# Turning q tiles, weights and part of the probability tiles through memory in a split-precision attention kernel

## The chip, the core and the metric

The kernel runs on one core of a Trainium2 chip. The metric is the device time of one execution, in microseconds (us). The engines work side by side, each through its own queue in order: PE (TensorE) multiplies matrices and can turn (transpose) a 128x128 tile into PSUM; DVE (VectorE), ACT (ScalarE) and POOL (GpSimd) work on elements; SP only issues DMAs and waits. Engines and DMAs tell each other through semaphores that a piece of work is done. P is 128, the number of partitions.

## The reference

Two layers on x of 2 batches, 1024 tokens and 512 features, in float32: an attention block with 32 query heads and 8 key/value heads of width 128, then a mixture of eight low-rank adapters. Cut to what matters:

```python
x = x + attn(layernorm(x), Wq, Wk, Wv, Wo, q_norm_w, k_norm_w)
x = x + ffn(layernorm(x), A, B, Wr, br)
# attn
q = rmsnorm((x @ Wq.T) by heads, q_norm_w);  k = rmsnorm((x @ Wk.T) by heads, k_norm_w);  v = x @ Wv.T by heads
scores = q @ k.T / sqrt(128);  bias = slope * (key - query), or -1e30 where key > query
out = softmax(scores + bias) @ v @ Wo.T
# ffn
gate = 8 * softmax(x @ Wr.T + br);  out = 2 * sum over h of gate[h] * (x @ A[h].T) @ B[h].T
```

The mask is causal: of the 8 key tiles of 128 tokens, query tile s needs s + 1.

## The kernel before

**Precision.** Each operand of a large product is split into two parts, hi (rounded to a format that PE multiplies fast, F32R) and lo (the remainder), and a product is three matmuls: hi by hi, lo by hi, hi by lo (`split_product`, L920).

**Windows.** A window w is one batch and one key/value head with its four query heads: 8 windows for batch 0, 8 for batch 1. In the text an A window is an ordinary one of batch 0 (list `GROUP_A`), a B window an ordinary one of batch 1 (`GROUP_B`); `PROLOGUE`, `BOUNDARY`, `FIRST_B` and `LAST` are the others. In a window, stage s (0 to 7) is one query tile of 128 tokens with all four heads: `q.s.c` makes q in four parts (c = 0 to 3), `scores.s.h` the scores of head h against s + 1 key tiles, `max`, `exp`, `invert` and `normalise` the softmax, `values.s.j` the product with the values of key tile j, `y.s` the product with Wo, `add_y` the sum into y. `kv` makes k and v of the next window. In A windows the weights of the next head are loaded and made ready (hi and lo, contraction index on the partitions) and a copy is kept in memory; B windows fetch that copy.

**Turning.** A matmul needs its contraction index on the partitions, so q, k, the probabilities, the layer norm's output and the weights are all turned: `turn` (L932) does four PE transposes of 128x128 into one PSUM bank `turn_ps` (a ring of three), `high` on ACT (L625, or L627 with a scale) writes the hi part from the bank, `low` on DVE (L801, or L803 with a scale) the lo part. I call the four transposes a set. Probabilities take 36 sets a window, q 8, and in A windows the weights 10 more (2 for Wk and Wv, 4 for Wq, 4 for Wo).

**Order.** The order on every engine comes from the six lists of names at the top (`turn.p.4.2`, `q.6.1`, ...): each engine walks the same lists and does those names that are its own, with the waits that each name's function has (`follow`). Nothing is chosen at run time. All large DMAs are issued by SP, in that order too.

**Buffers that matter here.** `probs` holds two stages of unnormalised, then normalised probabilities; `qn` one q tile; `s_ps` (two PSUM banks) the scores, so that `scores` of a head waits for the `max` one or two heads back; `turn_ps` three sets.

## Time and profile before

| | |
|---|---|
| median of 3 runs | 2194.55 us (2194.45 to 2194.65) |
| the profiled execution | 2194.96 us, of which the span is 2193.1 us |
| mean granted TensorE clock | 0.995 |
| PE busy | 97% of the span |
| HBM traffic | read 69.75 MB, written 46.14 MB, 53 GB/s over the span |
| instructions in the span | 33323 |

The span runs from the first to the last instruction that the profiler recorded. Busy time is the union of an engine's instructions; matmuls overlap one another, so the mean duration of one is longer than its share of the engine. The chain that ended last is the better price of a matmul: it gives each instruction only the time by which it moved the end. The table of instruction groups names a group by the first operands of its shape, and a "(+7 forms)" means that its mean mixes shapes. A DMA's time to landing is from its issue to the last semaphore.

### The profile page before, as it was taken

To read this page: it belongs to the slowest core of one execution; us is meant where nothing else is said; L and a number is where in the kernel's file an instruction comes from. 1 tells how busy PE (TensorE), PEld (TensorE's weight loads), DVE (VectorE), ACT (ScalarE), POOL (GpSimd) and SP (SyncE) were. 2 spreads that over 40 slices of the span, in tenths; PEclk is the share of its full clock that TensorE was granted. 3 is DMA by queue.
4 is the path that set the end of the run, shared out by engine and by line. 5 is a ranking of instruction groups with operands and counts; after the bars stand their busy time and mean duration, and the time that the engine had idled before them with its cause. 6 is when DMAs were issued, how large, how long until landed. Compare 5 with 4: busy or idle time off the path is not lost.

```text
span 2193.1 us, 33323 instructions
## 1 busy us (share of the span) xinstructions
PE 2135.6 (97%) x12220; PEld 1834.4 (84%) x12220; DVE 1373.7 (63%) x3431; ACT 1149.2 (52%) x3314; POOL 802.1 (37%) x872
## 2 busy tenths in 40 slices
PE   7999999999999999999999999999999999999997
PEld 6888888888888888888888888888888888888885
DVE  5656656566565666669766556565556656565686
ACT  3555555465554655545545455454545545455542
POOL 2433424244242433424424344342424424243341
PEclk9999999999999999999999999999999999999999
DMA  4212111121210212111121011101001111101100
GB/s 173 87 58 87 59 57 46 43 87 58 87 58 1 87 58 78 63 38 65 58 97 39 20 39 39 59 39 59 2 38 58 39 58 39 44 15 39 39 15 24
DMA packets 32129, 118.01 MB, mean 54 GB/s; under 512 B 4185, under 2 KB 4185, under 8 KB 23777
## 3 DMA queue, kind: packets, MB, share of 16 engines
q1 hardware_dynamic: 31536, 115.89, 14.1%
q8 instruction: 98, 1.61, 0.3%
q14 instruction: 63, 0.51, 0.1%
q10 hardware_dynamic: 432, 0.01, 0.0%
HBM read 69.75 MB, written 46.14 MB: 53 GB/s over the span
## 4 chain that ended last, share of the span: by engine, by line
PE 91%; DVE 4%; ACT 2%; issue 1%; POOL 1%; DMA 0%; ACTq 0%; POOLq 0%; DVEq 0%
PE s_ps L923 26%; PE o_ps L923 18%; PE y_ps L923 16%; PE turn_ps L990 15%; PE q_ps L923 15%; DVE kT_lo L803 1%; DVE pT_lo L801 1%; PE y_ps L1079 1%; DVE oT_lo L848 1%; ACT qn L641 0%; ACT kT_hi L627 0%; ACT oT_hi L660 0%; PE turn_ps L984 0%; ACT pT_hi L625 0%; DVE low_gated L896 0%
## 5 line engine op out<-in xcount | busy, mean ns | idle before, releaser
L717 POOL TENSOR_TENSOR probs<-probs,p_inv 128x896 f32<-128x896 f32 (+7 forms) x512 | 578.0, 1150 | 784.8 <-DVE p_inv L821 784.5
L632 ACT ACTIVATE probs<-probs,neg_max 128x896 f32<-128x896 f32 (+7 forms) x512 | 396.6, 777 | 295.5 <-DVE neg_max L814 293.4
L814 DVE CUSTOM_DVE_ANT_0 probs<-s_ps,rel 128x896 f32<-128x896 f32 (+7 forms) x512 | 382.9, 753 | 268.1 <-issue 266.9
L625 ACT ACTIVATE pT_hi<-turn_ps 128x512 fp32r<-128x512 f32 x576 | 332.0, 597 | 308.6 <-PE turn_ps L990 308.5
L801 DVE TENSOR_TENSOR pT_lo<-turn_ps,pT_hi 128x512 fp32r<-128x512 f32 x576 | 384.6, 685 | 139.9 <-ACT pT_hi L625 138.8
L990 PE MATMUL turn_ps<-ident,probs 128*128 128x128 f32 x2464 | 343.7, 273 | 4.3 <-DVE probs L837 2.5
L990 PEld LDWEIGHTS turn_ps<-ident,probs 128*128 128x128 f32 x2464 | 295.1, 141 | 54.0 <-issue 5.4
L923 PE MATMUL s_ps<-kT_hi,qT_hi 128*128 128x512 f32 (+3 forms) x768 | 278.7, 363 | 14.1 <-DVE kT_lo L803 12.5
L923 PE MATMUL s_ps<-kT_hi,qT_lo 128*128 128x512 f32 (+3 forms) x768 | 263.1, 343 | 0.0
L923 PE MATMUL s_ps<-kT_lo,qT_hi 128*128 128x512 f32 (+3 forms) x768 | 261.8, 341 | 0.0
L923 PE MATMUL o_ps<-pT_hi,v_hi 128*128 128x512 f32 x576 | 243.2, 422 | 1.8 <-DVE pT_lo L801 1.7
L923 PE MATMUL o_ps<-pT_lo,v_hi 128*128 128x512 f32 x576 | 226.1, 393 | 0.0
L923 PE MATMUL o_ps<-pT_hi,v_lo 128*128 128x512 f32 x576 | 226.0, 392 | 0.0
L923 PE MATMUL q_ps<-wqT_hi,xnT_hi 128*128 128x512 f32 x512 | 220.8, 431 | 2.1 <-DVE qn L825 2.1
L923 PE MATMUL y_ps<-woT_hi,oT_hi 128*128 128x512 f32 x512 | 203.7, 398 | 4.7 <-DVE oT_lo L848 3.9
L923 PE MATMUL q_ps<-wqT_hi,xnT_lo 128*128 128x512 f32 x512 | 202.8, 396 | 0.0
L923 PE MATMUL q_ps<-wqT_lo,xnT_hi 128*128 128x512 f32 x512 | 201.9, 394 | 0.0
L923 PE MATMUL y_ps<-woT_lo,oT_hi 128*128 128x512 f32 x512 | 200.1, 391 | 0.0
L923 PE MATMUL y_ps<-woT_hi,oT_lo 128*128 128x512 f32 x512 | 200.0, 391 | 0.0
L641 ACT ACTIVATE qn<-q_ps 128x128 f32<-128x128 f32 x512 | 134.8, 278 | 95.9 <-PE q_ps L923 92.8
L923 PEld LDWEIGHTS s_ps<-kT_hi,qT_hi 128*128 128x128 f32 x768 | 145.0, 189 | 39.1 <-DVE kT_lo L803 16.1
L923 PEld LDWEIGHTS s_ps<-kT_lo,qT_hi 128*128 128x128 f32 x768 | 145.4, 189 | 19.3 <-issue 1.0
(105 smaller groups left out, 3621.1 us busy)
## 6 DMA issues: line engine op xcount, KB each, us to landing
wq_raw<-in_L_attn_Wq SPq DMA_DIRECT2D x8, 1024.0 KB, 5.6
wo_raw<-in_L_attn_Wo SPq DMA_DIRECT2D x8, 1024.0 KB, 6.0
wq_kept<-wqT_hi SPq DMA_DIRECT2D x8, 1024.0 KB, 5.0
wq_kept<-wqT_lo SPq DMA_DIRECT2D x8, 1024.0 KB, 7.2
wo_kept<-woT_hi SPq DMA_DIRECT2D x8, 1024.0 KB, 7.0
wo_kept<-woT_lo SPq DMA_DIRECT2D x8, 1024.0 KB, 9.1
wqT_hi<-wq_kept SPq DMA_DIRECT2D x8, 1024.0 KB, 4.8
wqT_lo<-wq_kept SPq DMA_DIRECT2D x8, 1024.0 KB, 6.9
```

The source lines that it names most:

```text
L625: nc.scalar.activation(target, bank, ACT.Copy).then_inc(sems["high"], 1)
L632: nc.scalar.activation(row, row, ACT.Exp, bias=neg_max[:, s % 2, h:h + 1], scale=-1.0, accum_out=p_sum[:, s % 2, h:h + 1]).then_inc(sems[" ...
L641: last = nc.scalar.activation(qn[:, h, :], q_ps[:, h * HD:(h + 1) * HD], ACT.Square, scale=float(slopes[gg % NG * G + h]), accum_out=q_sum ...
L717: nc.gpsimd.tensor_tensor(row, row, p_inv[:, s % 2, h:h + 1].to_broadcast((P, L)), ALU.mult).then_inc(sems["normalise"], 1)
L801: nc.vector.tensor_tensor(target, bank, upper.bitcast(F32), ALU.subtract).then_inc(sems["low"], 1)
L803: nc.vector.scalar_tensor_tensor(target, bank, scale, upper.bitcast(F32), ALU.mult, ALU.subtract).then_inc(sems["low"], 1)
L814: nc.vector.tensor_tensor_reduce(out=probs[:, s % 2, h, 0:L], in0=s_ps[:, at_col:at_col + L], in1=rel[:, S - L:S], scale=-float(slopes[w % ...
L848: nc.vector.tensor_tensor(oT_lo[:].rearrange(flat), o_ps[:], oT_hi[:].rearrange(flat).bitcast(F32), ALU.subtract).then_inc(sems["o_low"], 1)
L923: last = nc.tensor.matmul(target, a, m, start=start and i == 0 and k == 0, stop=stop and i == len(pairs) - 1 and k == 2)
L990: last = nc.tensor.transpose(bank[0:width, i * rows:(i + 1) * rows], source, ident[0:rows, 0:rows])
L1079: nc.tensor.matmul(y_ps[:], low_turned[:, t % 2, :], bT[:], start=True, stop=True).then_inc(sems["f_out"], 1)
```

## The change

1. **q.** `turn.q`, `high.q` and `low.q` go. In their place SP writes `qn` to a buffer in memory (`send_q`, one DMA) and reads it back with four DMAs (`fetch_q`), each for 32 partitions, in runs of 32 floats (128 bytes), such that the 32x32 blocks stand where the turned tile wants them; DVE turns each 32x32 block in place (`flip_q`, one instruction for 128x512), ACT writes hi (`upper_q`), DVE lo (`lower_q`), now both from SBUF.
2. **Probabilities.** 15 of the 36 tiles of a window (`MEMORY_TILES`: the last ones of stages 2 to 7) take the same way: `send_p` (one DMA for each head, after its `normalise`), `fetch_p` (four DMAs for one or two tiles), `flip_p` on DVE, `upper_p` on ACT, `lower_p` on POOL. The values product takes them last. The other 21 tiles are turned by PE as before.
3. **Weights.** They are loaded from the inputs already in blocks: Wq in 4 DMAs and Wk and Wv in 8, in runs of 512 bytes, Wo in 16 DMAs in runs of 128 bytes. `flip_w` on DVE, `upper_w` on ACT and `lower_w` on POOL make them ready. The loads of Wq, Wk and Wv and all DMAs that keep or bring back weights are issued by ACT; Wo's by SP. The three raw buffers become one (`w_raw`), so that each load waits for another weight's `lower_w`.
4. **Buffers.** Two slots of turned and three of fetched probability tiles; `probs` in two tensors, for even and odd stages; `max` of a stage waits until the stage two before it has been sent.
5. **Order.** All six lists are new.

The core of the diff:

```diff
--- before.py
+++ after.py
+MEMORY_TILES = {2: ((2,),), 3: ((2, 3),), 4: ((3, 4),), 5: ((3, 4), (5,)), 6: ((4, 5), (6,)), 7: ((4, 5), (6, 7))}
...
-    "turn.wo.0 high.wo.0 turn.wo.1 norm_q.1 high.wo.1 scores.0.0 low.wo.0 scores.0.1 turn.wo.2 max.0.0 q.2.0 max.0.1 "
+    "load_w.wkv scores.0.0 scores.0.1 norm_q.1 max.0.0 send_q.1 max.0.1 q.2.0 exp.0.0 flip_w.wo.0 exp.0.1 scores.0.2 "
...
+    TURN_SLOTS, MEMORY_SLOTS, RAW_PAIRS = 2, 3, 2
...
+    def through_memory(s):
+
+        return [j for group in MEMORY_TILES.get(s, ()) for j in group]
+
+    def values_order(s):
+        return [j for j in range(s + 1) if j not in through_memory(s)] + through_memory(s)
 
...
-        probs = sb("probs", [P, 2, G, S])
+        probs = [sb("probs_even", [P, G, S - P]), sb("probs_odd", [P, G, S])]
-        pT_hi = sb("pT_hi", [P, RING, G * P], F32R)
-        pT_lo = sb("pT_lo", [P, RING, G * P], F32R)
+        q_raw = sb("q_raw", [P, G * P])
+        p_raw = sb("p_raw", [P, 2 * RAW_PAIRS, G * P])
+        pT_hi = sb("pT_hi", [P, TURN_SLOTS + MEMORY_SLOTS, G * P], F32R)
+        pT_lo = sb("pT_lo", [P, TURN_SLOTS + MEMORY_SLOTS, G * P], F32R)
...
+        q_bounce = nc.dram_tensor("q_bounce", [2, G, P, HD], F32).ap()
+        p_bounce = nc.dram_tensor("p_bounce", [2, NT, G, P, P], F32).ap()
...
+            def send_q(w, n):
+                gg, s = w + n // NT, n % NT
+                unit = number["send_q", gg, s] - 1
+                if unit >= 2:
+                    sp.wait_ge(sems["flip_q"], unit - 1)
+                after(sp, "norm_q", gg, s)
+                sp.dma_start(q_bounce[unit % 2].rearrange("h p d -> p h d"), qn[:]).then_inc(q_sent, 16)
+
+            def fetch_q(w, n):
+                unit = number[named(w, "fetch_q", n)] - 1
+                sp.wait_ge(q_sent, 16 * (unit + 1))
+                if unit:
+                    sp.wait_ge(sems["lower_q"], unit)
+                blocks = q_bounce[unit % 2].rearrange("h (a j) (b i) -> b j (h a) i", j=BLOCK, i=BLOCK)
+                for b in range(NBLK):
+                    sp.dma_start(q_raw[b * BLOCK:(b + 1) * BLOCK, :].rearrange("p (n i) -> p n i", i=BLOCK),
+                                 blocks[b]).then_inc(q_fetched, 16)
+
+            def send_p(w, s, h):
+                first = through_memory(s)[0]
...
+                after(sp, "normalise", w, s, h)
+                sp.dma_start(p_bounce[s % 2, first:s + 1, h].rearrange("u p c -> p u c"),
+                             probs[s % 2][:, h, first * P:(s + 1) * P].rearrange("p (u c) -> p u c", c=P)).then_inc(p_sent[s % 2], 16)
+            def fetch_p(w, s, j):
+                ring, value = fetched[w, s, j]
+                sp.wait_ge(p_sent[s % 2], sent[w, s])
...
+                n = len(next(g for g in MEMORY_TILES[s] if g[0] == j))
+                blocks = p_bounce[s % 2, j:j + n].rearrange("u h (a j) (b i) -> b j (u h a) i", j=BLOCK, i=BLOCK)
+                for b in range(NBLK):
+                    sp.dma_start(p_raw[b * BLOCK:(b + 1) * BLOCK, 2 * ring:2 * ring + n, :].rearrange("p u (n i) -> p (u n) i", i=BLOCK),
+                                 blocks[b]).then_inc(p_fetched[ring], 16)
...
+            wo_v = Wo.rearrange("(n i) (g h a j) -> g h a i n j", i=BLOCK, h=G, a=NBLK, j=BLOCK)
+
+            def load_w(w, of):
+                if of == "wo" and w + 1 < NG:
+                    after(sp, "lower_w", "wq", w + 1, C - 1)
+                    for h in range(G):
+                        for a in range(NBLK):
+                            sp.dma_start(w_raw[a * BLOCK:(a + 1) * BLOCK, h, :].rearrange("i (n j) -> i n j", j=BLOCK),
+                                         wo_v[w + 1, h, a]).then_inc(wo_loaded, 16)
+
...
+                g = w + 1
+                if g >= NG or of == "wo":
+                    return
+                if of == "wkv":
+                    if g:
+                        after(act, "lower_w", "wkv", g - 1, 1)
+                    for a in range(NBLK):
+                        rows = w_raw[a * BLOCK:(a + 1) * BLOCK, G:G + 2, :].rearrange("i m (n k) -> i m n k", n=NBLK)
+                        act.dma_start(rows[:, 0], wk_v[g, a]).then_inc(wkv_loaded, 16)
+                        act.dma_start(rows[:, 1], wv_v[g, a]).then_inc(wkv_loaded, 16)
+                else:
+                    if g:
+                        after(act, "lower_w", "wo", g - 1, G - 1)
+                    for a in range(NBLK):
+                        rows = w_raw[a * BLOCK:(a + 1) * BLOCK, 0:G, :].rearrange("i h (n k) -> i (h n) k", n=NBLK)
+                        act.dma_start(rows, wq_v[g, a]).then_inc(wq_loaded, 16)
+
...
+            def upper_q(w, n):
+                gg, s = w + n // NT, n % NT
+                after(act, "flip_q", gg, s)
+                if s >= 2 or gg:
+                    after(act, "scores", gg - (s < 2), (s - 2) % NT, G - 1)
+                nc.scalar.activation(qT_hi[:, s % 2].rearrange("p h n -> p (h n)"), q_raw[:], ACT.Copy,
+                                     scale=wq_norm[:]).then_inc(sems["upper_q"], 1)
+
+            def upper_p(w, s, j):
+                after(act, "flip_p", w, s, j)
+                if p_before[w, s, j]:
+                    after(act, "values", *p_before[w, s, j])
+                nc.scalar.activation(pT_hi[:, values_slot(w, s, j), :], p_raw[:, p_raw_slot[w, s, j], :],
+                                     ACT.Copy).then_inc(sems["upper_p"], 1)
+
...
+            def lower_p(w, s, j):
+                r = values_slot(w, s, j)
+                after(pool, "upper_p", w, s, j)
+                nc.gpsimd.tensor_tensor(pT_lo[:, r, :], p_raw[:, p_raw_slot[w, s, j], :], pT_hi[:, r, :].bitcast(F32),
+                                        ALU.subtract).then_inc(sems["lower_p"], 1)
+
+            def lower_w(w, of, i):
+                after(pool, "upper_w", *named(w, "upper_w", of, i)[1:])
+                upper, target, source = weight_part(of, i)
+                nc.gpsimd.tensor_tensor(target, source, upper.bitcast(F32), ALU.subtract).then_inc(sems["lower_w"], 1)
+
...
+            def flip_q(w, n):
+                unit = number[named(w, "flip_q", n)]
+                dve.wait_ge(q_fetched, 16 * NBLK * unit)
+                nc.vector.transpose(q_raw[:], q_raw[:]).then_inc(sems["flip_q"], 1)
+
+            def lower_q(w, n):
+                gg, s = w + n // NT, n % NT
+                flat = "p h n -> p (h n)"
+                after(dve, "upper_q", gg, s)
+                nc.vector.scalar_tensor_tensor(qT_lo[:, s % 2].rearrange(flat), q_raw[:], wq_norm[:],
+                                               qT_hi[:, s % 2].rearrange(flat).bitcast(F32), ALU.mult,
+                                               ALU.subtract).then_inc(sems["lower_q"], 1)
+
+            def flip_p(w, s, j):
+                ring, value = fetched[w, s, next(g for g in MEMORY_TILES[s] if j in g)[0]]
+                dve.wait_ge(p_fetched[ring], value)
+                raw = p_raw[:, p_raw_slot[w, s, j], :]
+                nc.vector.transpose(raw, raw).then_inc(sems["flip_p"], 1)
+
...
+                if h == 0:
+                    earlier = (w, s - 2) if s >= 2 else (w - 1, s + NT - 2)
+                    if earlier in sent:
+                        dve.wait_ge(p_sent[s % 2], sent[earlier])
...
-                elif of == "q":
-                    after(pe, "norm_q", w + which[0] // NT, which[0] % NT)
-                    sources = [qn[:, h, :] for h in range(G)]
...
-                    after(pe, "low", "q", w, s)
+                    after(pe, "lower_q", w, s)
...
-                r = piece(s, j) % RING
-                after(pe, "low", "p", w, s, j)
+                r = values_slot(w, s, j)
+                if j in through_memory(s):
+                    after(pe, "lower_p", w, s, j)
+                else:
+                    after(pe, "low", "p", w, s, j)
                 split_product(o_ps[:], [((v_hi[:, j, :], v_lo[:, j, :]), (pT_hi[:, r, :], pT_lo[:, r, :]))],
-                              start=j == 0, stop=j == s).then_inc(sems["values"], 1)
+                              start=j == order[0], stop=j == order[-1]).then_inc(sems["values"], 1)```

What the engines' programs show at three places. `x3` at a row's end means three such instructions; in brackets the semaphores that the row waits for.

PE in the first A window, from q of tile 2 (`turn_ps<-ident,qn` turns it) to the first scores of stage 2 (the `128x384` row). Before:

```order
L990 MATMUL turn_ps<-ident,qn 128x128 [waits norm_q_done,low_done]
L990 MATMUL turn_ps<-ident,qn 128x128 x3
L923 MATMUL q_ps<-wqT_hi,xnT_hi 128x512
L923 MATMUL q_ps<-wqT_lo,xnT_hi 128x512
L923 MATMUL q_ps<-wqT_hi,xnT_lo 128x512
L923 MATMUL q_ps<-wqT_hi,xnT_hi 128x512
L923 MATMUL q_ps<-wqT_lo,xnT_hi 128x512
L923 MATMUL q_ps<-wqT_hi,xnT_lo 128x512
L923 MATMUL q_ps<-wqT_hi,xnT_hi 128x512
L923 MATMUL q_ps<-wqT_lo,xnT_hi 128x512
L923 MATMUL q_ps<-wqT_hi,xnT_lo 128x512
L923 MATMUL s_ps<-kT_hi,qT_hi 128x384 [waits max_done,low_done]
```

The change, the rows up to the same scores (the q products are those of tile 4):

```order
L1106 MATMUL q_ps<-wqT_lo,xnT_hi 128x512
L1106 MATMUL q_ps<-wqT_hi,xnT_lo 128x512
L1106 MATMUL q_ps<-wqT_hi,xnT_hi 128x512
L1106 MATMUL q_ps<-wqT_lo,xnT_hi 128x512
L1106 MATMUL q_ps<-wqT_hi,xnT_lo 128x512
L1106 MATMUL q_ps<-wqT_hi,xnT_hi 128x512
L1106 MATMUL q_ps<-wqT_lo,xnT_hi 128x512
L1106 MATMUL q_ps<-wqT_hi,xnT_lo 128x512
L1106 MATMUL q_ps<-wqT_hi,xnT_hi 128x512
L1106 MATMUL q_ps<-wqT_lo,xnT_hi 128x512
L1106 MATMUL q_ps<-wqT_hi,xnT_lo 128x512
L1106 MATMUL s_ps<-kT_hi,qT_hi 128x384 [waits max_done,lower_q_done]
```

The set is gone, the scores wait for `lower_q_done` instead, and PE has been given q of tiles 3 and 4 ahead of them, where it had only q of tile 3.

SP in the first A window, around the load of Wo. Before, one DMA for Wo and the two that keep it:

```order
L522 DMA wq_kept<-wqT_hi 128x2048 [waits low_done]
L523 DMA wq_kept<-wqT_lo 128x2048
L513 DMA wo_raw<-in_L_attn_Wo 128x4x512 [waits turn_done]
L527 DMA wo_kept<-woT_hi 128x2048 [waits low_done]
L528 DMA wo_kept<-woT_lo 128x2048
```

The change (the `x15` row is the rest of the 16 loads of Wo):

```order
L586 DMA q_raw<-q_bounce 32x16x32 [waits lower_q_done,q_sent]
L586 DMA q_raw<-q_bounce 32x16x32 x3
L648 DMA w_raw<-in_L_attn_Wo 32x16x32 [waits lower_w_done]
L648 DMA w_raw<-in_L_attn_Wo 32x16x32 x15
L595 DMA p_bounce<-probs_even 128x3x128 [waits normalise_done,flip_p_done]
L595 DMA p_bounce<-probs_even 128x3x128 [waits normalise_done] x3
L608 DMA p_raw<-p_bounce 32x32x32 [waits lower_p_done,p_sent_even]
L608 DMA p_raw<-p_bounce 32x32x32 x3
```

The sends of stage 6 (`128x3x128`) stand behind the 16 loads on the one SP queue.

DVE in the first A window, at the first scores of stage 4 (`128x640`). Before:

```order
L854 TENSOR_TENSOR y<-y_ps,y 128x512 [waits y_done,y_loaded1]
L736 MEMSET scratch 128x1 [waits scores_done]
L814 ISA probs,neg_max<-s_ps,rel 128x512
L814 ISA neg_max 128x1
L821 RECIPROCAL p_inv<-p_sum 128x2 [waits exp_done]
L803 SCALAR_TENSOR_TENSOR qT_lo<-turn_ps,wq_norm,qT_hi 128x512 [waits high_done]
```

The change:

```order
L1003 TENSOR_TENSOR qn<-q_ps,q_inv 128x512 [waits inv_q_done]
L999 RECIPROCAL p_inv<-p_sum 128x2 [waits exp_done]
L943 TENSOR_TENSOR pT_lo<-turn_ps,pT_hi 128x512 [waits high_done]
L999 RECIPROCAL p_inv<-p_sum 128x2 [waits exp_done]
L966 STREAM_TRANSPOSE p_raw<-p_raw 128x512 [waits p_fetched0]
L1034 TENSOR_TENSOR y<-y_ps,y 128x512 [waits y_done,y_loaded1]
L894 MEMSET scratch 128x1 [waits scores_done,p_sent_even]
L992 ISA probs_even,neg_max<-s_ps,rel 128x640
```

A wait for a DMA (`p_fetched0`) now stands on DVE ahead of `add_y` and of the `max` of stage 4.

## Rows read from the trace of the kernel before

**Rows 1.** The page: engines' busy us, share of the span, instructions.

```profile
PE 2135.6 (97%) x12220; PEld 1834.4 (84%) x12220; DVE 1373.7 (63%) x3431; ACT 1149.2 (52%) x3314; POOL 802.1 (37%) x872
```

**Rows 2.** The chain that ended last, share of the span by line.

```profile
by line: PE s_ps L923 26.1%; PE o_ps L923 17.5%; PE y_ps L923 16.1%; PE turn_ps L990 15.4%; PE q_ps L923 15.3%; issue 1.2%; DVE kT_lo L803 0.7%; DVE pT_lo L801 0.6%; PE y_ps L1079 0.6%; DVE oT_lo L848 0.5%; ACT qn L641 0.5%; ACT kT_hi L627 
```

**Rows 3.** Windows, one A and one B: stretch, length, busy us by engine, clock, DMA.

```profile
177.75:310.38 132.63, 131.66 (x766) 113.84 (x765) 82.37 (x199) 73.24 (x209) 48.46 (x51) 1.00 0.16 60
1389.80:1519.77 129.97, 127.50 (x724) 109.72 (x725) 76.73 (x189) 68.17 (x200) 48.44 (x50) 1.00 0.11 41
```

**Rows 4.** Chain that ended last, stretch 1258 to 1300: start, us, what.

```profile
1270.35 1.15 ACT qn L641 x8
...
1278.66 2.76 PE y_ps L923 x12
1281.42 0.68 PE o_ps L923 x3
1282.10 1.07 PE s_ps L923 x6
1283.16 0.44 PE turn_ps L990 x4
1283.60 0.69 PE q_ps L923 x3
```

**Rows 5.** The same chain, stretch 0 to 66.

```profile
46.20 0.21 POOL q_sum_eps L690
46.48 1.02 POOL q_inv L692
47.52 0.70 DVE qn L825
...
55.34 0.36 PE s_ps L923 x3
```

**Rows 6.** Instruction groups by shape: busy us, mean ns, idle before.

```profile
L801 DVE TENSOR_TENSOR pT_lo<-turn_ps,pT_hi 128x512 fp32r<-128x512 f32 x576 | 384.6, 685 | 139.9 <-ACT pT_hi L625 138.8
...
L717 POOL TENSOR_TENSOR probs<-probs,p_inv 128x1024 f32<-128x1024 f32 x64 | 119.9, 1896 | 143.5 <-DVE p_inv L821 143.5
...
L803 DVE SCALAR_TENSOR_TENSOR qT_lo<-turn_ps,wq_norm,qT_hi 128x512 fp32r<-128x512 f32 x128 | 95.7, 748 | 37.5 <-ACT qT_hi L627 37.1
...
L627 ACT ACTIVATE qT_hi<-turn_ps,wq_norm 128x512 fp32r<-128x512 f32 x128 | 88.1, 688 | 41.6 <-PE turn_ps L990 41.3
...
L814 DVE CUSTOM_DVE_ANT_0 probs<-s_ps,rel 128x1024 f32<-128x1024 f32 x64 | 78.1, 1220 | 53.1 <-issue 53.1
...
L632 ACT ACTIVATE probs<-probs,neg_max 128x1024 f32<-128x1024 f32 x64 | 73.6, 1150 | 21.9 <-DVE neg_max L814 21.9
...
L717 POOL TENSOR_TENSOR probs<-probs,p_inv 128x512 f32<-128x512 f32 x64 | 65.7, 1048 | 76.8 <-DVE p_inv L821 76.8
...
L751 DVE TENSOR_SCALAR probs<-y,x_moment,x_inv 128x512 f32<-128x512 f32 x8 | 4.3, 539 | 0.1
```

**Rows 7.** DMA over the span: packets, MB, share of 16 engines; two times to landing.

```profile
q1 hardware_dynamic: 31536, 115.89, 14.1%
...
out<-y SPq DMA_DIRECT2D x16, 256.0 KB, 2.0
...
wkv_raw<-in_L_ffn_B SPq DMA_DIRECT2D x1, 256.0 KB, 4.1
```

**Rows 8.** DMA, 977 to 982 us: load of B, 1024 runs of 256 bytes.

```profile
DMA  0000000000094688999964110000000000000000
q1 hardware_dynamic: 1040, 0.26, 23.7%
```

**Rows 9.** DMA, 1021 to 1023.3 us: a store of y, 128 runs of 2 KB.

```profile
q1 hardware_dynamic: 144, 0.26, 30.3%
```

**Rows 10.** SP's queue, 720 to 731 us: start, us of the issue.

```profile
720.14 0.33 SPq L498 DMA_DIRECT2D wkv_raw<-in_L_attn_Wk  x1
720.52 1.73 SPq L499 DMA_DIRECT2D wkv_raw<-in_L_attn_Wv  x1
```

325 lines of the change are left out of this document (168 added, 157 removed), and 496 rows, old and new, of tables (BOUNDARY, FIRST_B, GROUP_A, GROUP_B).

## The prediction

> **What bounds the kernel now.** I read the busy times first. PE is busy 97% of the span, the next engine (DVE) 63%, POOL 37% [rows 1]. The chain that ended last says the same in another way: nearly all its large entries are PE's, and `turn_ps` L990, PE's transposes, is 15.4% of it [rows 2]. The stretches of one window show how little PE waits: 132.63 us long with PE busy 131.66 in an A window, 129.97 with 127.50 in a B window; DVE is at 62% and 59%, ACT at 55% and 52%, the DMA engines at 16% and 11% of their time, at full clock [rows 3]. So the end moves with PE's work, for as long as the others bring its operands in time.
>
> **What the change removes from PE.** Transposes overlap one another and the matmuls beside them, so I price them by the chain: a set of four is 0.44 us [rows 4]. Out go 128 sets of q (16 windows by 8), 240 of probabilities (16 by 15), and 80 of weights (8 by 10): 448 sets, 197.1 us. The other price: 15.4% of 2193.1 is 338 us [rows 2] for the 848 sets that the lists hold (46 a window for probabilities, q and k, 80 for weights, 32 for the layer norms), 0.398 each, 178 us for those that go. I take 197, since the set in rows 4 is one of these, between two matmuls of 512 columns; 178 stays as the lower end. An A window loses 33 sets (14.5 us), a B window 23 (10.1 us). That gives a span of 2193.1 - 197.1 = 1996.0.
>
> **What it adds.** No operation of the new way is in this trace, so each gets bounds from the nearest rows.
>
> The 32x32 transpose on DVE (448 instructions of 128x512): between 0.54 us (a copy from SBUF with a scale) and 0.75 (`qT_lo`); I take 0.65, near the many 128x512 rows [rows 6]. An A window adds 33 x 0.65 = 21 us and gives 25 lo parts at 0.685 (17 us) to POOL; DVE stays at about 86 of 119 us. A B window: +15.0 - 10.3, about 81 of 120. POOL takes a lo part at between 1.05 (L717 at 512 columns) and 1.90 (its price at 1024 columns, if a full second operand counts like twice the columns) [rows 6]; at 1.05 POOL comes to 48.5 + 26 = 75 us in an A window, at 1.90 to 96. Both fit. ACT's hi parts only change their source. ACT also issues 18 DMAs in an A window: 0.33 to 1.73 us each, the second end where the queue is full [rows 10]; 6 to 31 us, I take 9, with 83 us of ACT in all. All this lies beside PE's work, which is 118 us in an A window (132.63 - 14.5). If that cover is gone (an engine in order waits while PE wants its result), it comes back as waits, below.
>
> The DMA engines. A window moves 47104 runs of 128 bytes (q 16384, probabilities 30720), an A window 8192 more for Wo. The price of a run: the load of B took 23.7% of 16 engines for 5 us over 1040 packets, 18.2 ns for 256 bytes [rows 8]; a store of y 30.3% over 2.3 us for 128 packets of 2 KB, 87 ns [rows 9]. A line through both gives 8.4 ns and 0.0384 ns a byte: 13.3 ns at 128 bytes, 28 at 512. The ends are 8.4 (no bytes) and 36 (twice the 256-byte price, if a short run pays double); I take 13.3. In an A window each engine then has 3456 short runs (46 us), 928 of 512 bytes from the sends and the loads of Wq, Wk, Wv (26 us), and 5.24 MB of kept weights (13 us): 85 of 118 us. In a B window 2944 short (39), 736 of 512 bytes (21) and 13: 73 of 120. That is 72% and 61%, against 16% and 11% now: room, but no longer empty queues. The load of B also shows the supply holding near 9 tenths of all engines [rows 8].
>
> Waits. A q tile used to go, after its last product: squares 1.15, inverse root 0.21 + 1.02, norm 0.70, set 0.44, hi 0.69, lo 0.75 [rows 4 to 6], 5.0 us plus handing over. Now it has, after the norm (3.1 in all), the send 2.0 (as for the store of y), four fetches of which the last is issued 1.2 us after the first and lands some 2.5 later (between 2.0 for the store and 4.1 for B, a quarter of its size) [rows 7], flip 0.65, hi 0.69, lo 0.75, and about 0.8 for eight handovers: 11.7 us. PE's work between the last q product of tile 2 and the first scores of stage 2 is the tightest place of a B window: a set 0.44, values 0.68, four q parts 2.76, y 2.75, four scores of stage 1 at 0.35, four q parts 2.76, together 10.8 [rows 4, 5]; in the order shown for PE one sees the last of them. So about 1 us is missing there in each window, half that at its neighbours, and 0.5 for chance lateness: 2 us a window. Queued behind the q wait on DVE (`flip_q`) are `max`, `add_y` and the lo parts, and PE's next scores wait for `max` since `s_ps` has two banks.
>
> A probability tile of stage 7 needs, after the last scores: `max` 1.2, `exp` 1.15 and its sum 0.2, inverse 0.2, two normalises 3.8, send 2.4, fetch of a pair 1.2 + 2.9 (256 short runs per engine are 3.4, of which part lies under the issues), flip, hi and lo 0.65 + 0.6 + 1.05, handovers 0.6: 15.9 us [rows 6, 7]. PE has some 18.7 us of work before it (16.2 in the last window), 21 to 27 at the other tiles: this is covered, with 3 us to spare at the tightest. It costs nothing while the queue adds under 3 us. In A windows the 16 loads of Wo stand ahead of stage 6's sends: 512 short runs per engine, 6.8 us of the one queue; and ACT is held by its issues. Stage 6 has 26 us for some 17 of need, so most is covered; I take 2 us a window more. Taken: 4 us for each A window, 2 for each B window, 48 in all, between 0 (all covered) and 8 and 6 (112, each engine's in-order wait reaching PE in full at two to three stages). Prologue and last window keep their own waits; PE's 3 us less in the prologue I leave against the 12 DMAs for the first weights.
>
> The sum: 1996 + 48 = 2044 for the span, 1.9 around it, 2046; the profiled execution is 0.4 above the median, so 2045.5, and I say 2045. Without the waits 1998, with all of them 2110.
>
> `lower_q` reads two SBUF tensors while POOL works at its own; before, its first operand was in PSUM. No row shows the pair, and I take nothing for it.
> The Trainium skill has a rule that speaks against this (SBUF — State Buffer, "Who interferes with whom"): a DVE instruction with two SBUF inputs and a GpSimd instruction that reads SBUF shut each other out for the whole instruction. By it about half of the 128 would wait some 0.5 us, 32 us of DVE, and with half of that on q's path the sum would be 2061 instead of 2045, inside the forecast's own range.
>
> **The rivals.**
>
> *Fully covered.* The order gives enough work ahead of each late operand, and no queue grows: 1998. For it: PE's own waits are 1 to 2.5 us a window now [rows 3], though the old q chain was as long as its lead. Against it: the 10.8 against 11.7 us above.
>
> *Waits on DMA in DVE's queue.* `flip_p` and `flip_q` stand in DVE's order where they are due and not later; each late landing holds `max` and so `s_ps`. With 1.5 us at five of eight stages, 7 us a window: 1996 + 112 + 2 = 2110. For it: queues at 60 to 70% and one queue in order. Against it: DVE idle a third of the time, which catches up.
>
> *The DMA engines become the bound: slower than before.* Where a 128-byte run costs x ns, an A window needs 3456 x + 38.6 us and a B window 2944 x + 33.2. Both together reach the old 262.6 us at x = 30 ns; from there on the kernel is slower. At the upper end of 36 ns they are 163 and 139 us: 2195 + 8 x (30.4 + 9.4) = 2510. For it: reads and writes of so many short runs, each DMA to 32 partitions only, are in no row. Against it: 18.2 ns for twice the bytes [rows 8].
> The Trainium skill speaks for this rival (DMA: Bandwidth & Descriptors, Specifications): at least 512 bytes are wanted for full rate, and below that the engine reads, changes and writes. The load of B, at 256 bytes, does not show a doubling: 18.2 ns lie below the 87 ns of 2 KB by nearly the bytes' share plus a constant.
>
> That the change does not do what it says I exclude: the engines' programs show the sets gone.
>
> **How the numbers follow.** Forecast (2020 to 2075) 0.42; covered (below 2020) 0.20; waits on DMA (2075 to 2190) 0.21; DMA bound 0.15, nearly all above 2199; 0.02 for between. A measurement of this kernel tells 0.2% (4.4 us) from no change: faster 0.83, same 0.02, slower 0.15. The range that leaves out two tenths: the covered case down to 1990 (1998 is the lowest that I can price, less some of PE's own waits), and upwards the waits up to 2150; out stay DMA bound and the worst of the waits. The forecast's own range is 2020 to 2075.
>
> **What would show it.** Right: PE busy near 1940 us of a span near 2044; a window of 118 to 123 us; `turn_ps` at about 140 us of the chain; short packets at 12 to 16 ns and a DMA share of 60 to 75%; PE's idle time before `s_ps` with `qT_lo` as releaser, 1 to 2 us a window, and little before `o_ps`. DVE's transpose near 0.65, POOL's lo part near 1.05. Wrong: q or probability fetches landing 6 us or more after issue, a DMA share above 90%, or POOL's lo part near 1.9 us, which would put 0.85 us into each late tile.

## The result, and the profile after

The changed kernel takes 2326.21 us in the median of 4 runs (2321.77 to 2329.12), the kernel before 2194.5 beside it (2191.93 to 2194.65): ratio 1.0601, 95% interval 1.0582 to 1.0621. Forecast were 2045 us, range 1990 to 2150. It is slower, by more than any of the cases but the one of the DMA bound, and that one is not what happened.

The profiled execution has a span of 2323.4 us. Its busy times, against [rows 1]:

```profile
PE 2037.6 (88%) x10428; PEld 1688.3 (73%) x10428; DVE 1499.2 (65%) x3559; ACT 1181.4 (51%) x3314; POOL 1236.8 (53%) x1192
```

PE has 98.0 us less to do than before and is idle 285.8 us where it was idle 57.5. So 228 us of new idle time stand against 98 us of work gone. The chain that ended last was nine tenths PE's before [rows 2]; now it is, by engine and by line:

```profile
PE 27%; DVE 16%; DMA 16%; SPq 14%; POOL 10%; issue 10%; ACT 5%; ACTq 1%; DVEq 0%
PE o_ps L1106 7%; PE y_ps L1106 7%; SPq L608 6%; PE s_ps L1106 6%; PE q_ps L1106 5%; POOL probs_odd L864 4%; DMA p_raw<-p_bounce 4%; DMA q_bounce<-qn 4%; DMA q_raw<-q_bounce 3%; SPq L586 3%; SPq L648 3%; DMA p_bounce<-probs_odd 3%; DVE pT_lo L943 3%; DVE qT_lo L958 2%; PE turn_ps L1159 2%
```

Transfers and SP's issues of them are 30% of it. One A and one B window, in the columns of [rows 3]:

```profile
355.90:502.80 146.90, 126.77 (x633) 105.02 (x634) 91.86 (x207) 76.91 (x210) 83.06 (x75) 0.94 0.59 137
1405.00:1534.60 129.60, 121.26 (x634) 101.53 (x634) 83.54 (x197) 68.95 (x201) 68.09 (x65) 0.97 0.57 135
```

The A window has grown from 132.63 to 146.9 us, the B window has only kept its length, no engine is full, and the granted clock, 1.00 before, is 0.94 and 0.97 (the numbers ahead of the DMA share). What PE waited for (us in total, times, longest):

```profile
PE o_ps L1106 <- DVE pT_lo L943: 80.3, 35, 7.9
PE s_ps L1106 <- DVE qT_lo L958: 76.2, 24, 6.1
PE s_ps L1106 <- DVE neg_max L992: 31.8, 31, 5.1
PE turn_ps L1159 <- DVE probs_odd L909: 17.0, 3, 10.2
```

The largest is not for a tile that came through memory: L943 makes the low part of a tile that PE turned itself. The chain at the start of a B window shows how a transfer gets there (start, us, what):

```profile
1392.83 0.62 DVE qn L1003
...
1393.51 6.84 DMA q_bounce<-qn
...
1400.43 1.14 ACT qn L786 x8
1401.58 0.50 ACT pT_hi L730
...
1402.10 0.70 DVE pT_lo L943
...
1402.93 1.62 PE o_ps L1106 x3
```

The store of q takes 6.84 us to land. `qn` is one buffer, so ACT's squares of the next q wait for it, in ACT's queue behind them stands `pT_hi`, and PE stands at `o_ps`. The clock falls to 0.50, the level of 1.2 GHz, at 1400.6, while it stands, and is back at 1.00 at 1407.5, within the third stretch below (the clock is the first number after the busy times):

```profile
1398.00:1402.00 4.00, 0.00 (x0) 0.00 (x0) 0.00 (x0) 1.57 (x9) 0.27 (x2) 0.83 0.51 160
1402.50:1404.50 2.00, 1.57 (x4) 1.31 (x5) 1.16 (x3) 0.00 (x0) 0.44 (x1) 0.50 0.43 71
1404.60:1408.70 4.10, 4.10 (x13) 3.21 (x13) 1.80 (x3) 1.20 (x2) 0.00 (x0) 0.65 0.43 96
1409.00:1412.00 3.00, 3.00 (x17) 2.54 (x15) 0.70 (x3) 0.90 (x8) 1.21 (x2) 1.00 0.21 33
```

The DMA queues in that stretch, 1393 to 1404 us (packets, MB, share of 16 engines):

```profile
DMA  9229999999989999589979864000004769776723
q10 hardware_dynamic: 286, 2.04, 49.1%
q1 hardware_dynamic: 2640, 0.52, 22.9%
```

q10 is ACT's queue with the 3 MB of Wk, Wv and Wo that come back, 2.04 MB of them in this stretch: the 16 engines are at 9 tenths for most of the first half. A packet of these, 7.1 KB in the mean, holds an engine for 302 ns. In A windows the same happens with the weights that are kept and Wq that is loaded:

```profile
373.50 8.55 DMA q_raw<-q_bounce
```

This fetch of q lands after 8.55 us (2.3 in the median), and `flip_q` stands in DVE's queue for it, with `max` behind it. ACT is held at the same time, by the issues of its four loads of Wq, with `exp` behind them (start, us):

```profile
374.20 6.38 ACTq L685 DMA_DIRECT2D w_raw<-in_L_attn_Wq  x4
```

### The profile page after: what moved, and what is told of

Its sections match the earlier page's. It is cut to its first block, busy times and chain, and to the rows that moved or that the text cites. A ratio compares the mean times of both kernels' runs of the same rounds, so it can differ in the third digit from the quotient of the medians.

```text
span 2323.4 us, 32916 instructions
## 1 busy us (share of the span) xinstructions
PE 2037.6 (88%) x10428; PEld 1688.3 (73%) x10428; DVE 1499.2 (65%) x3559; ACT 1181.4 (51%) x3314; POOL 1236.8 (53%) x1192
## 2 busy tenths in 40 slices
DMA packets 1082765, 311.06 MB, mean 134 GB/s; under 512 B 852056, under 2 KB 1065048, under 8 KB 1074400
## 3 DMA queue, kind: packets, MB, share of 16 engines
q10 hardware_dynamic: 40368, 96.49, 11.9%
## 4 chain that ended last, share of the span: by engine, by line
PE 27%; DVE 16%; DMA 16%; SPq 14%; POOL 10%; issue 10%; ACT 5%; ACTq 1%; DVEq 0%
PE o_ps L1106 7%; PE y_ps L1106 7%; SPq L608 6%; PE s_ps L1106 6%; PE q_ps L1106 5%; POOL probs_odd L864 4%; DMA p_raw<-p_bounce 4%; DMA q_bounce<-qn 4%; DMA q_raw<-q_bounce 3%; SPq L586 3%; SPq L648 3%; DMA p_bounce<-probs_odd 3%; DVE pT_lo L943 3%; DVE qT_lo L958 2%; PE turn_ps L1159 2%
## 5 line engine op out<-in xcount | busy, mean ns | idle before, releaser
L864 POOL TENSOR_TENSOR probs_odd<-probs_odd,p_inv 128x256 f32<-128x256 f32 (+3 forms) x256 | 327.0, 1300 | 251.4 <-DVE p_inv L999 251.4
L870 POOL TENSOR_TENSOR pT_lo<-p_raw,pT_hi 128x512 fp32r<-128x512 f32 x240 | 311.0, 1314 | 229.5 <-ACT pT_hi L753 229.1
L864 POOL TENSOR_TENSOR probs_even<-probs_even,p_inv 128x128 f32<-128x128 f32 (+3 forms) x256 | 271.3, 1083 | 226.1 <-DVE p_inv L999 226.1
L1106 PE MATMUL s_ps<-kT_hi,qT_hi 128*128 128x512 f32 (+3 forms) x768 | 286.3, 373 | 110.5 <-DVE qT_lo L958 76.2
L1106 PE MATMUL o_ps<-pT_hi,v_hi 128*128 128x512 f32 x576 | 245.1, 425 | 83.3 <-DVE pT_lo L943 80.3
L775 ACT ACTIVATE probs_odd<-probs_odd,neg_max 128x256 f32<-128x256 f32 (+3 forms) x256 | 211.8, 832 | 180.4 <-DVE neg_max L992 126.7
L943 DVE TENSOR_TENSOR pT_lo<-turn_ps,pT_hi 128x512 fp32r<-128x512 f32 x336 | 222.0, 680 | 95.5 <-ACT pT_hi L730 94.4
L1106 PE MATMUL s_ps<-kT_hi,qT_lo 128*128 128x512 f32 (+3 forms) x768 | 271.3, 353 | 0.0
L1106 PEld LDWEIGHTS s_ps<-kT_hi,qT_hi 128*128 128x128 f32 x768 | 150.6, 196 | 165.7 <-DVE qT_lo L958 93.6
L1106 PE MATMUL s_ps<-kT_lo,qT_hi 128*128 128x512 f32 (+3 forms) x768 | 270.3, 352 | 0.0
L775 ACT ACTIVATE probs_even<-probs_even,neg_max 128x128 f32<-128x128 f32 (+3 forms) x256 | 184.8, 722 | 138.0 <-DVE neg_max L992 137.3
L753 ACT ACTIVATE pT_hi<-p_raw 128x512 fp32r<-128x512 f32 x240 | 147.4, 632 | 203.3 <-DVE p_raw L966 182.1
L966 DVE STREAM_TRANSPOSE p_raw<-p_raw 128x512 f32<-128x512 f32 x240 | 159.3, 692 | 132.8 <-DMA p_raw<-p_bounce 132.3
L730 ACT ACTIVATE pT_hi<-turn_ps 128x512 fp32r<-128x512 f32 x336 | 192.9, 594 | 95.4 <-PE turn_ps L1159 95.0
L1106 PE MATMUL q_ps<-wqT_hi,xnT_hi 128*128 128x512 f32 x512 | 221.1, 432 | 17.7 <-DVE qn L1003 12.0
L992 DVE CUSTOM_DVE_ANT_0 probs_odd<-s_ps,rel 128x256 f32<-128x256 f32 (+3 forms) x256 | 207.3, 820 | 36.8 <-issue 36.2
L1106 PE MATMUL o_ps<-pT_lo,v_hi 128*128 128x512 f32 x576 | 230.6, 400 | 0.0
L1106 PE MATMUL o_ps<-pT_hi,v_lo 128*128 128x512 f32 x576 | 230.2, 400 | 0.0
L992 DVE CUSTOM_DVE_ANT_0 probs_even<-s_ps,rel 128x128 f32<-128x128 f32 (+3 forms) x256 | 173.8, 686 | 70.2 <-issue 68.9
L786 ACT ACTIVATE qn<-q_ps 128x128 f32<-128x128 f32 x512 | 134.0, 276 | 167.0 <-PE q_ps L1106 104.8
L1106 PE MATMUL y_ps<-woT_hi,oT_hi 128*128 128x512 f32 x512 | 204.8, 400 | 10.0 <-POOL woT_lo L876 6.1
L1106 PE MATMUL q_ps<-wqT_lo,xnT_hi 128*128 128x512 f32 x512 | 209.0, 408 | 0.0
## 6 DMA issues: line engine op xcount, KB each, us to landing
q_bounce<-qn SPq DMA_DIRECT2D x128, 256.0 KB, 2.4
p_bounce<-probs_odd SPq DMA_DIRECT2D x64, 256.0 KB, 2.5
w_raw<-in_L_attn_Wq ACTq DMA_DIRECT2D x32, 256.0 KB, 8.9
```

Of the source, the lines that this page charges most:

```text
L730: nc.scalar.activation(pT_hi[:, values_slot(w, *which), :], bank, ACT.Copy).then_inc(sems["high"], 1)
L753: nc.scalar.activation(pT_hi[:, values_slot(w, s, j), :], p_raw[:, p_raw_slot[w, s, j], :], ACT.Copy).then_inc(sems["upper_p"], 1)
L775: nc.scalar.activation(row, row, ACT.Exp, bias=neg_max[:, s % 2, h:h + 1], scale=-1.0, accum_out=p_sum[:, s % 2, h:h + 1]).then_inc(sems[" ...
L786: last = nc.scalar.activation(qn[:, h, :], q_ps[:, h * HD:(h + 1) * HD], ACT.Square, scale=float(slopes[gg % NG * G + h]), accum_out=q_sum ...
L864: nc.gpsimd.tensor_tensor(row, row, p_inv[:, s % 2, h:h + 1].to_broadcast((P, L)), ALU.mult).then_inc(sems["normalise"], 1)
L870: nc.gpsimd.tensor_tensor(pT_lo[:, r, :], p_raw[:, p_raw_slot[w, s, j], :], pT_hi[:, r, :].bitcast(F32), ALU.subtract).then_inc(sems["lowe ...
```

## The experiments

17 kernels ran. An A window is the mean of windows 1 to 7, a B window that of 9 to 15, from one `v_lo` product to the next in the profiled execution. The ratio is to the kernel before, on the same chip.

```
                      us      ratio (95%)              A      B     PE busy  idle
before             2194.5                           133.8  130.9   2135.6    58
changed            2326.2  1.0601 (1.0582-1.0621)   147.4  132.4   2037.6   286
w_by_pe            2323.7  1.0588 (1.0572-1.0604)   150.1  130.4   2057.3   266
p_by_pe            2382.4  1.0855 (1.0839-1.0871)   144.4  142.1   2129.7   251
q_by_pe            2331.3  1.0621 (1.0605-1.0637)   146.2  134.8   2079.6   248
all_by_pe          2417.3  1.1023 (1.1005-1.1042)   146.5  144.1   2193.7   219
light_kept         2175.5  0.9916 (0.9899-0.9932)   137.1  123.6   1996.6   170
light_wide         2144.6  0.9774 (0.9759-0.9789)   134.5  123.4   1990.2   153
light_wide_two_qn  2154.7  0.9816 (0.9798-0.9834)   135.9  123.2   1990.4   163
before_light       2193.8  0.9996 (0.9987-1.0006)   133.8  130.9   2135.5    56
kept_512B          2326.5  1.0603 (1.0587-1.0619)   149.1  131.6   2040.7   283
kept_2KB           2309.7  1.0529 (1.0502-1.0556)   145.7  131.6   2031.3   270
paced              2311.9  1.0542 (1.0526-1.0558)   146.3  132.9   2032.2   279
paced_w_by_pe      2313.1  1.0557 (1.0525-1.0588)   146.9  132.9   2067.5   244
two_qn             2312.3  1.0551 (1.0517-1.0585)   148.2  129.6   2040.4   266
two_qn_paced       2304.8  1.0517 (1.0486-1.0548)   145.5  132.1   2040.6   262
whole_rows         2311.5  1.0525 (1.0501-1.0549)   145.8  131.5   2029.6   270
q_no_wait          2303.0  1.0503 (1.0487-1.0518)   147.7  130.5   2037.1   264
lower_p_on_dve     2375.7  1.0822 (1.0785-1.0859)   152.8  133.6   2057.1   320
```

### One part undone

In each, `flip`, `upper`, `lower` of the part become `turn`, `high`, `low` in the lists, through the three PSUM banks, and its sends and fetches go:

```diff
-flip_w.wo.0 ... upper_w.wo.0 ... lower_w.wo.0     (w_by_pe; p_by_pe and q_by_pe alike)
+turn.wo.0 high.wo.0 low.wo.0
```

> The changed kernel with one part undone: Wq, Wk, Wv and Wo are loaded in whole rows (4 DMAs for a group instead of 28) and turned by TensorE as before (80 sets, 80 x 0.44 = 35 us of PE work put back); q tiles and 15 of 36 probability tiles still go through memory. Theory weights (the weights' many small loads on ACT's and SP's queues and the stretch that they give q's trip cost the A windows their 146 us against 131 in B windows): A windows fall to about 128, the prologue gains some 10, B windows stay at 131; 2325 - 7 x 18 - 10 = about 2190. Theory trip (the trip of q and p through memory is longer than its lead, with or without the weights): A windows keep 146 and gain 4 us of PE work each that partly fills the waits; 2300 to 2350. Theory DVE (DVE's queue standing at a flip delays the low parts of tiles that PE turned): DVE loses ten flips a window but not the waits, 2290 to 2340.

> The changed kernel with one part undone: all 36 probability tiles of a group are turned by TensorE (240 sets, 106 us of PE work put back); q and the weights still go through memory. Theory trip/q (PE stands for q): the waits for qT_lo stay and the sets fill waits for pT_lo; 2325 + 106 - 80 (the waits for pT_lo) = about 2350. Theory DVE (p's flips wait for DMAs in DVE's queue and hold the low parts): those 132 us of DVE waits go and with them the 80 us of PE's and part of the half clock; 2300 to 2330. Theory weights: A windows stay some 15 us above B windows; about 2390.

> The changed kernel with one part undone: q tiles are turned by TensorE (128 sets, 56 us of PE work put back); the weights and the 15 probability tiles still go through memory. Theory trip/q (q's trip of 12 us and more against a lead of 11 us is what PE waits for most): 76 us of waits for qT_lo and as much time at half clock and in held queues go, 2325 + 56 - 170 = about 2210. Theory DVE (p's flips are what holds): about 2325 + 56 - 60 = 2320. Theory weights: A windows stay 15 us above B windows, about 2330.

> All three parts undone (q, probabilities and weights turned by TensorE), but with the changed kernel's order of work, slots and queues (loads and kept weights on ACT's queue). It says what the new order costs by itself. Theory latency (the transfers are what costs): close to the kernel before, 2195 to 2215, A windows 134, B windows 131. Theory order (the new lists are worse whatever is turned where): above 2250.

None gives the time back. With the weights turned by PE the time stays, though PE is busy 19.7 us more, and the A windows even grow (147.4 to 150.1): their short loads and flips cost about what the 80 sets do, and they are not what makes the A window 13 us long. With q by PE it is 2331, with p by PE 2382. No named theory fits both the time and the windows: 2382 is nearest to the 2390 of the weights theory, but A and B windows are 144.4 and 142.1 there and not 15 apart. Undoing all three gives 2417, 223 us more than the kernel before with the same work. Its largest waits of PE:

```profile
PE s_ps L1105 <- DVE neg_max L991: 69.8, 80, 1.7
PE q_ps L1105 <- DVE qn L1002: 36.9, 34, 3.2
```

So the lists of the change, without their transfers, are no version of the kernel before. I put each set where its tile was due, which is later than a good order would; how much of the 223 us is my placement and how much the new order is not told apart. What the undone kernels do say is that taking out one part alone recovers nothing, so no one of the three holds the loss by itself.

### The bytes of the kept weights

```diff
-act.dma_start(target[0], hi[:].rearrange(flat).bitcast(F32)).then_inc(spilled, 16)
+n = target[0].shape[1] // 16
+act.dma_start(target[0][:, 0:n], hi[:].rearrange(flat)[:, 0:n].bitcast(F32)).then_inc(spilled, 16)
```

The lo parts and the DMAs that bring the weights back are shortened in the same way, so the second half computes with other weights.

> The changed kernel, but of the turned weights only one sixteenth of each row is written to memory in the first half and brought back in the second (what stays in SBUF is used instead, so the second half computes with other weights); every instruction, wait and DMA issue stays. It takes away 3 MB of each window's bulk transfers. Theory bulk (one fetch of q in each A window and one store in each B window lands after 8 to 10 us instead of 2.3, because megabytes of weights pass the same DMA engines, and PE then stands and falls to half clock): A windows 146 to 136 or less, B windows 131 to 124; 2325 - 7 x 8 - 8 x 7 = about 2210. Theories trip, DVE and issue: within 1% of 2325.

This is the run that moves: 2175.5, 151 us less, 0.8% below the kernel before. It is below the forecast of its own theory, 2210. A windows lose 10.3 us, which hold only the keeping, and B windows 8.8, which hold only the bringing back. Its queues over the span, and one A and one B window:

```profile
q1 hardware_dynamic: 1042224, 212.47, 47.7%
q10 hardware_dynamic: 40368, 17.84, 3.4%
```

```profile
326.90:464.20 137.30, 123.09 (x633) 101.95 (x633) 91.26 (x206) 76.63 (x211) 83.22 (x75) 0.98 0.54 110
1300.00:1424.00 124.00, 119.60 (x627) 99.95 (x626) 82.83 (x196) 69.00 (x199) 67.64 (x65) 0.99 0.49 101
```

q1's packets are the same, q10's bytes fall from 96.49 to 17.84 MB, and the clock is back at 0.98 and 0.99. The late landings go with the bytes: in the changed kernel 7 of the 56 stores of q in the seven A windows and 9 of the 56 in the seven B windows land after more than 6 us, and 10 of the 224 fetches of q in A windows; with light weights it is 1, 0 and 0. The same edit in the kernel before (SP's queue there) is the control:

> The kernel before, with one sixteenth of the kept weights' bytes moved (the second half computes with what stays in SBUF). Theory bytes before trips (megabytes of weights cost time only as they delay q's and p's trips, and here there are none): 2190 to 2195, no change. Theory bytes as such (writing to and reading from SBUF at 300 GB/s slows the engines): 2100 to 2150.

No change: 0.9996 (0.9987 to 1.0006), though its queue falls from 115.89 MB [rows 7] to a third:

```profile
PE 2135.5 (97%) x12220; PEld 1835.5 (84%) x12220; DVE 1373.3 (63%) x3431; ACT 1147.8 (52%) x3314; POOL 800.8 (37%) x872
q1 hardware_dynamic: 31536, 37.25, 5.3%
```

So the kept bytes cost nothing in the kernel without q and p in the queues, and 151 us in the one with them. By which way they cost, late landings, ACT's longer issues or the sum of bytes, this pair does not say.

### In which form the bytes cost

```diff
-wq_kept = nc.dram_tensor("wq_kept", [NG, 2, P, C * W512], F32).ap()
+wq_kept = nc.dram_tensor("wq_kept", [NG, 2, C * W512 // FINE, P, FINE], F32).ap()   # FINE 128 or 512
```

> The changed kernel with the kept weights laid out in memory in pieces of 128 numbers, so that keep and back move the same bytes as 512-B packets where they were whole rows of 4 and 8 KB (in the stretch 1393 to 1404 the queue of the kept weights ran 272 packets, 1.97 MB, in 44.1% of 16 engines: 285 ns a packet). Nothing else changes. Theory turns (the DMA engines take packets from the two queues in turn, so each short packet of q's trip waits for one long packet of weights: 32 packets per engine of a store against 24 long ones of the 3 MB, which is the whole 8 us): a store beside the weights lands after 32 x (28 + 28) ns + 2 = about 4 us and a fetch after 128 x (13 + 28) ns + 2 = about 7 us; B windows fall by about 6 us, A windows by 5, total about 2325 - 90 = 2235. Theory bytes (the stretch is simply so many bytes ahead in the engines): at 28 ns for 512 B the same 3 MB takes 10.5 us instead of 8.5, so nothing is gained or it gets slower: 2325 to 2350.

> As the run before it in the list, with pieces of 512 numbers (2-KB packets, 87 ns each by the stores of y). Theory turns: a store beside the weights has 32 x (28 + 87) ns + 2 = 5.7 us, a fetch 128 x (13 + 87) ns: the whole of the bulk's 8 us as now; between the changed kernel and the 512-B one, about 2290. Theory bytes: no difference from 2325.

```diff
-keep_wo load_w.wq norm_q.3 ...
+keep_wo.0 load_w.wq norm_q.3 ... (10 items) ... keep_wo.1 ...   # paced: 256 KB each
```

> The changed kernel with the same bytes of kept weights, all kept and all brought back, but in pieces of 256 KB, one every 3 us or so of ACT's order (one every 1 us where they are wanted soon), and Wk/Wv brought back 60 places later: 40 DMA issues on ACT's queue in a window instead of 6. Theory queued bytes (what costs is 1 to 3 MB handed over at once, 8 us of all 16 engines, in front of q's store or fetch): no transfer of q lands after more than 4 us, and most of the 150 us that leaving out the bytes gave comes back: 2180 to 2230. Theory share (what costs is the sum of bytes in a window, not when they go): 2310 to 2340. Theory issue (ACT's queue pays 0.35 to 0.45 us for each DMA): 34 more issues a window are 13 us of ACT, of which a part shows: up to 2400.

> As the run before, with the weights loaded in whole rows and turned by TensorE (80 sets, some 27 us more PE work; 24 fewer short-packet DMAs a window). Theory queued bytes: with the loads of w_by_pe the A windows also lose the 2 to 3 us a window that whole rows gave beside the light kept weights; 2180 to 2220, equal to the run before within 20 us.

Pieces of 512 B: nothing, but not cleanly. ACT's wait for `qn` halves (50.0 to 25.4 us), and its issue of a lo part of Wq grows from 0.45 to 2.29 us:

```profile
L691 ACTq DMA_DIRECT2D wq_kept<-wqT_lo x8: 1878/2286/2467, 32.7 to 1036.0; - x8
```

Pieces of 2 KB give 16 us, spreading 14 (and 13 with the weights turned by PE). What came out is what the other theories said: no gain from 512 B (2325 to 2350), and 2310 to 2340 for `paced` if the sum of bytes costs and not when they go. In B windows the spreading was not as wide as its text says: Wo has to be back before `y.0`, about the fiftieth of the list's 491 items, so its 2 MB still went out within 10 us (1509.4 to 1519.0), and beside them

```profile
1511.20 7.14 DMA q_bounce<-qn
```

13 of the 56 stores of q in B windows still land after more than 6 us, so for B windows the run does not tell the burst from the sum of bytes. In A windows Wo's eight pairs of pieces are 11 items apart, and Wq's too; fetches of q over 6 us fall from 10 to 1 and its stores from 7 to 5, and ACT's idle time at its issues from 53.1 to 25.1 us. Yet the A window is only 1.1 us shorter, where leaving the bytes out gave 10.3. So the burst is not shown to be the cost there: nearly all of the cost stays when the bytes come spread out. By which way it does is open; `paced` also has 34 more issues a window on ACT.

### Single waits

> The changed kernel, but the fetch of q reads a fixed part of x and does not wait until the store of q has landed, so the scores are computed with other numbers. Every instruction and byte stays; q's trip is shorter by the store's landing (2.4 us in the median, 9 us where it passes beside the kept weights). Theory trip (PE waits for the end of q's trip, which is late by the transfers): A and B windows fall by the late landing, 5 to 7 us each; 2325 - 15 x 6 = about 2235. Theory DVE (PE waits because DVE's queue stands at other flips): less than 15 us of change.

```diff
-sp.wait_ge(q_sent, 16 * (unit + 1))
-blocks = q_bounce[unit % 2].rearrange("h (a j) (b i) -> b j (h a) i", j=BLOCK, i=BLOCK)
+blocks = x[n % 2, 0:4 * P, 0:P].rearrange("(h a j) (b i) -> b j (h a) i", h=G, j=BLOCK, i=BLOCK)
```

> The changed kernel with two qn buffers in turn, so that ScalarE's squares and DVE's product for the next q tile don't wait until the store of the last one has landed. SBUF was full; the room comes from the tables of the LoRA part, halved and read twice (other numbers come out, every instruction keeps its shape but three copies at the start). Theory qn (in a B window the chain of waits goes store of q 6.84 us, then ScalarE's squares, pT_hi, pT_lo, PE; ScalarE waits 50 us for it in sum, half a dozen us a window): B windows fall by 5 to 6 us to about 126, A windows by 1 to 2; 2325 - 8 x 5.5 - 8 = about 2270. Theory fetch (the fetch of the late q is then the next thing that is late, and the scores that need it wait as long): B windows by 2 at most, 2305 or more.

```diff
-qn = sb("qn", [P, G, HD])
+qn = sb("qn", [P, 2, G, HD])
-act.wait_ge(q_sent, 16 * (number["send_q", gg, s] - 1))
+act.wait_ge(q_sent, 16 * (number["send_q", gg, s] - 2))
```

> As two_qn, with the kept weights moved in pieces of 256 KB spread over the window. In the paced run q's stores still landed after 7 to 8.5 us once a window and held ScalarE. Theory qn: with both, the late stores are hidden and no fetch lands late: 2200 to 2240. Theory bytes (each transfer that passes beside weights is late by a little, and there are many): 2290 to 2310, as paced.

> The changed kernel, all bytes kept and brought back, but the weights loaded in whole rows with 4 DMAs a group instead of 28, so that the flips turn other blocks than the weights' (other numbers come out). Theory ACT issue (ScalarE stands 8.5 us a window at its issues for Wq behind the kept weights, SyncE 16 issues for Wo): A windows fall by 6 to 9 us, B windows stay: 2325 - 60 = about 2265. Theory bytes (beside the light weights it was worth 2.6 us an A window and 31 us in all): 2290 to 2300.

```diff
-for a in range(NBLK):
-    act.dma_start(rows, wq_v[g, a]).then_inc(wq_loaded, 16)
+act.dma_start(w_raw[:, 0:G, :], wq_v[g]).then_inc(wq_loaded, 16)
```

They give 14 to 23 us, about a quarter of what the theory that is named first in each text gave (a fifth for two_qn_paced); the two kernels with two buffers are where the second theory of their texts had them. The profile's waits that end with a transfer show where the time goes (us in total; the last column is ACT's idle time ahead of `exp` of an odd stage, where it stands at its own DMA issues):

```
                 p flip on DVE  q flip on DVE  squares on ACT  issue on ACT
changed              132.3          69.6           50.0            53.1
q_no_wait            120.6          49.1           49.2            44.9
two_qn               126.6         101.4            -              51.4
whole_rows           109.9          66.3           55.8            16.2
paced                134.6          74.8           53.7            25.1
light_kept            79.5          15.9           12.0            20.3
light_wide            64.0          15.5           14.5             7.6
```

With two buffers the squares don't wait any more, and DVE's flip of q takes over (69.6 to 101.4), whose queue holds `max` and the low parts just as ACT's did:

```profile
DVE p_raw L969 <- DMA p_raw<-p_bounce: 126.6, 74, 5.4
DVE q_raw L955 <- DMA q_raw<-q_bounce: 101.4, 41, 7.3
```

q_no_wait lowers all four by 41 us in sum, for 23 of time; taking the bytes away lowers them by 177, for 151. whole_rows takes ACT's idle time at its issues from 53.1 to 16.2, as far as light_kept does, and gives 15 us: that share alone is small.

> The run with one sixteenth of the kept bytes (2175), and in addition Wq, Wk, Wv and Wo loaded in whole rows, 4 DMAs a group instead of 28, so that the flips turn other blocks than the weights': output is not the reference's. What is left of the difference between the halves there (A windows 137.1 us, B windows 123.6) is put to the loads. Theory issue (ScalarE stands up to 3.9 us a window at its 12 DMA issues and SyncE 7 us at 16, and the short packets fill the engines): A windows fall by 8 to 12 us to about 127, 2175 - 7 x 10 - 5 = about 2100. Theory vector (the weights' ten flips, ten upper and ten lower parts on DVE, ACT and POOL hold the attention's own work in those queues): no more than 2 us a window, about 2160.

> The changed kernel with one sixteenth of the kept bytes, the weights loaded in whole rows and two qn buffers, that is all three of the costs found, taken away together. Theory transfers (these are all of the excess but the 50 us that TensorE's sets were worth less than priced): 2144 - 14 = 2130, from 1996 + 50 = 2046 still 84 away, which would be the chain of q and p itself, DVE's, ScalarE's and GpSimd's steps. Rival: without the long landings the wait for the buffer was hidden, no change from 2144.

Beside light weights whole rows are worth 31 us (23 between the profiled executions, with 2.6 in each A window, a third of what the issue theory gave or less). Two buffers on top cost 10 us; that the wait was hidden where the store lands in time would explain no gain, and not these 10. Together, bytes and short loads are 2326.2 - 2144.6 = 182 us.

### Low parts on DVE

> The changed kernel with the 240 low parts of the probability tiles that came through memory computed on VectorE instead of GpSimd (1.31 us each there, 315 us in sum; 0.7 to 1.1 us on DVE). Theory shared port (while GpSimd reads and writes SBUF, DVE's two-input instructions wait: the low part of q took 1128 ns instead of 748): DVE's other instructions get shorter and it gains, 2290 to 2320. Theory DVE full (DVE at 65% has no room in the order, and its queue stands at flips): 240 x 0.7 = 170 us more in its queue, 2340 to 2400.

```diff
-nc.gpsimd.tensor_tensor(pT_lo[:, r, :], p_raw[:, p_raw_slot[w, s, j], :], pT_hi[:, r, :].bitcast(F32),
+nc.vector.tensor_tensor(pT_lo[:, r, :], p_raw[:, p_raw_slot[w, s, j], :], pT_hi[:, r, :].bitcast(F32),
```

49 us slower: it was right to give them to POOL. That DVE has no 0.7 us to spare at that place in its queue is the likely reason; PE's idle time is 34 us more. The durations (min/median/max) of the low parts with two inputs from SBUF, and of those with one in PSUM:

```profile
L965 DVE TENSOR_TENSOR pT_lo<-p_raw,pT_hi x240: 646/682/2002, 110.4 to 2356.9; 128x512 fp32r<-128x512 f32 x120
L937 DVE TENSOR_TENSOR pT_lo<-turn_ps,pT_hi x336: 650/681/710, 68.3 to 2349.4; 128x512 fp32r<-128x512 f32 x168
```

48 of the 240 ran while POOL worked, and they took 836 ns in the median and up to 2002; the other 192 took at most 694. The second kind stays under 0.71 us with POOL at work (192 of them) and without.

No version ran that gives the reference's output and beats the kernel before: light_kept and light_wide leave bytes out.

## Why the prediction was wrong

**What PE loses: mis-sized.** 448 sets at 0.44 were 197.1 us, 178 the lower end. Measured are 98.0 us in the changed kernel. With the bytes and the short loads out of the way PE is busy 1990.2 us against 2135.6: 145.4 us, 0.32 a set, below both prices.

Part of the shortfall is the clock. By the trace's clock records PE was busy at the lower level for 16 us in the kernel before, 44 in light_wide and 142 in the changed kernel. Counting all products at their full-clock length (an estimate from their times from start to next start; a matmul of `o_ps` is 242 ns there and 437 at the lower level), PE's work falls by about 155 to 160 us in both: 0.35 a set. The other products keep their length (a matmul of `o_ps` 241 ns before and 242 after, of `s_ps` 162 and 161), but a transpose takes 98.6 ns before and 107.9 after: the sets that are left got dearer, 0.39 to 0.43. And all_by_pe, with the new order and all sets, has PE busy 2193.7 us, 58 more than the kernel before with the same work, of which the lower clock is some 17 to 20. Against that order the sets are worth what was forecast: 2193.7 less the 1996.6 of light_kept is 197.1. So the price of a set held only against the new order; against the kernel before, the new order made part of PE's remaining work dearer, and the forecast had that at nothing.

Put back by parts into the changed kernel, a set was 19.7 / 80 = 0.25 (weights), 42.0 / 128 = 0.33 (q), 92.1 / 240 = 0.38 (p); these are differences in busy time, too, and PE's time at the lower level falls in each (142 to 133, 122 and 105 us).

**What is added on the engines: sizes nearly right.** Flip 0.69 (p) and 0.71 (q) against 0.65, POOL's low part 1.31 against 1.05:

```profile
L966 DVE STREAM_TRANSPOSE p_raw<-p_raw 128x512 f32<-128x512 f32 x240 | 159.3, 692 | 132.8 <-DMA p_raw<-p_bounce 132.3
L870 POOL TENSOR_TENSOR pT_lo<-p_raw,pT_hi 128x512 fp32r<-128x512 f32 x240 | 311.0, 1314 | 229.5 <-ACT pT_hi L753 229.1
L958 DVE SCALAR_TENSOR_TENSOR qT_lo<-q_raw,wq_norm,qT_hi 128x512 fp32r<-128x512 f32 x128 | 144.4, 1128 | 11.5 <-ACT qT_hi L746 11.2
```

The engines' sums fit beside PE as forecast: in the A window above DVE is busy 91.9 us (86 forecast), ACT 76.9 (83), POOL 83.1 (75). `qT_lo`, which I left at its old 748 ns, takes 1128 in the mean. Its fastest is 703 and its slowest 1860, and what runs beside it decides: the 33 of 128 beside which POOL all but stood still took 731 to 753 ns, the other 95 1265 in the median. The trace agrees with the rule that I had cited and priced inside the range (the Trainium skill, SBUF — State Buffer, "Who interferes with whom"): a DVE instruction with two SBUF inputs contends with a GpSimd instruction that reads SBUF. 128 x 0.38 = 49 us of DVE, not of time.

**The DMA engines: price right.** Packets by size, and the queues of SP and ACT, over the span:

```profile
DMA packets 1082765, 311.06 MB, mean 134 GB/s; under 512 B 852056, under 2 KB 1065048, under 8 KB 1074400
q1 hardware_dynamic: 1042224, 212.47, 44.6%
q10 hardware_dynamic: 40368, 96.49, 11.9%
```

q1's packets took 15.9 ns each; my prices of 13.3 ns for the 852056 short ones and 28 for the rest give 16.0. The share is 59% and 57%, below the 72 and 61 forecast, since the windows are longer. The kernel is slower, yet not by the rival of the DMA bound: at 13.3 ns a run the engines need 85 of an A window's 147 us. The rule beside that rival (the Trainium skill, DMA: Bandwidth & Descriptors, Specifications) does not show as a doubled price in these packets.

**The waits: the step that failed.** It said "Taken: 4 us for each A window, 2 for each B window, 48 in all, between 0 (all covered) and 8 and 6 (112)". Measured are 228 us of new idle time. The median landings were as taken: store 2.4 (2.0), fetch 2.3 (2.5), probability pair 3.0 (2.9). What was left out is what the kept weights cost the transfers beside them. I had their 13 us in the sum of the engines' time and found room for them, and put nothing for them into the waits. With 15/16 of their bytes gone PE is idle 170.0 us instead of 285.8, and the run is 151 us shorter. One way is seen in the trace: they come as 2 to 3 MB at once, and for 8 us what is issued beside them lands late, at least once in every window: 6.84 and 8.55 us above. An average share of 60% says nothing on that. Whether this is most of the 151 is not shown; the A windows of `paced` make it doubtful. The working listed the landing of 6 us as a sign of being wrong, and did not price it.

The second omission is the in-order queue on ACT. The working priced ACT's 18 issues at 9 us and laid them "beside PE's work". It missed that `square_q` now waits on a store (`q_sent`) because there is one `qn` buffer, which had been freed by PE 0.44 us after the norm. The rival of waits in DVE's queue had the right shape, with 1.5 us at five stages; it had neither this wait nor the bytes.

From the base, by the runs: 2193.1 - 145.4 (PE's work gone) + 95.7 (new idle time that stays in light_wide) = 2143.4; + 180.0 for the bytes and short loads (132.6 idle, 47.4 of PE's busy time, about what 98 us more at the lower clock cost) = 2323.4. By the medians 151 of them go with the kept bytes and 31 with the short loads. So even without either the time is 100 us above the forecast of 2045: 52 of PE's work and 48 of waits. The 95.7 have no experiment of their own. In light_wide PE waits 37.7 us for `pT_lo` of L938, 16.5 for `neg_max` and 15.9 for `qn`: the longer chains of the new order, as all_by_pe suggests; that is argued and not shown.

## What to carry to other kernels

Before an operand is sent through memory, list every bulk transfer that shares its DMA engines, and price the operand's landing beside the largest of them, not by the median and not by the mean share: here 2.3 us became 7 to 9 in every window, and taking those bytes away gave 151 us. Spreading them out is no substitute by itself: it gave 14. Then list the buffers that the transfer now frees late and the in-order queues in which somebody waits for them; taking one such wait away gave 14 to 23 us here, with the next in its place. And a set's price in the old chain (0.44) is not yet what its removal saves: PE's busy time fell by 0.32 a set, since the lower clock and the new order took part of it back.

## What was not expected of the hardware

- Big packets and small ones do share the engines, but the small ones pay: beside 2 to 3 MB on ACT's queue, a 256-KB store on SP's queue lands after 6.5 to 9.5 us instead of 2.4, once in every A and B window.
- Cutting the same bytes into 512-B packets raises their share of the 16 engines from 11.9% to 15.2% and the issue of one 1-MB DMA on ACT from 0.45 to 2.29 us.
- A DMA that fetches to 32 partitions with 128-B runs takes SP 0.49 us (q) and 0.56 us (a pair of probability tiles) in the median to issue, 3.3 us at the most; such issues are 9% of the chain (L608 and L586), the landings of these fetches 7%.
- The 32x32 transpose of 128x512 takes 0.66 to 0.72 us for Wo, q and the probabilities, and 1.08 to 1.16 for Wq, Wk and Wv, whose view of the buffer has a stride. Their hi parts on ACT take 1.16 us as well (Wq, median), against 0.62 for Wo's, which is read without one.
